# A decoder layer on one core: cross scores in two passes instead of three, and expert blocks issued among the last batches' steps

## The reference

```python
x = x + attn(layernorm(x), W_qkv, W_out)              # causal, window 64
x = x + xattn(layernorm(x), ctx, Wq, Wkv, Wo, bias)   # ctx: 375 rows per batch, bias by relative position
x = x + ffn(layernorm(x), ...)                        # 8 experts of width 512, top 2
# xattn: scores = q @ k.T + bias; softmax; @ v; @ Wo
# ffn: probs = softmax(x @ router.T), top 2 kept and renormalised
#      y = sum_e probs_e * ((silu(x @ gate_e + b) * (x @ up_e + b)) @ down_e + b)
```

## Time and profile before

| | us |
|---|---|
| median of three runs | 1296.43 |
| the profiled execution | 1294.94 |
| its span, first to last instruction | 1293.2 |
| PE busy | 1221.5 (94%) |
| DVE busy | 869.6 (67%) |
| POOL busy | 851.0 (66%) |
| ACT busy | 726.3 (56%) |

### The profile page before, as it was taken

One profiled execution on the slowest core, in us unless ns is written; L12 is line 12 of the kernel. 1 busy time (PEld: TensorE's weight loads), 2 busy tenths in 40 slices (PEclk: granted clock), 3 DMA queues, 4 the chain that ended last, 5 costly groups with the idle time before them and its releaser, 6 DMA issues. The chain is left out here.

```text
span 1293.2 us, 39996 instructions
## 1 busy us (share of the span) xinstructions
PE 1221.5 (94%) x13786; PEld 1084.2 (84%) x13787; DVE 869.6 (67%) x3942; ACT 726.3 (56%) x1822; POOL 851.0 (66%) x1595
## 2 busy tenths in 40 slices
PE   6899999999999999999999999996199999999996
PEld 4688888888888888888888888885199999999996
DVE  3567778787787877888778787786344444444443
ACT  3466666666666666666666666664054444444442
POOL 4677787887878878778787887765434444444443
PEclk8999999999999999999999999998599999999998
DMA  8700011100110111100111110101377322233222
GB/s 165 134 21 22 28 39 44 29 29 28 39 44 29 28 29 39 44 29 29 29 39 44 29 28 24 33 16 30 126 217 180 50 48 44 47 49 49 49 46 25
DMA packets 43957, 66.22 MB, mean 51 GB/s; under 512 B 6833, under 2 KB 30769, under 8 KB 43793
## 3 DMA queue, kind: packets, MB, share of 16 engines
q1 hardware_dynamic: 27808, 38.93, 11.4%
q0 software_dynamic: 15552, 25.05, 10.0%
q10 hardware_dynamic: 432, 0.10, 0.0%
HBM read 43.10 MB, written 20.95 MB: 50 GB/s over the span
## 5 line engine op out<-in xcount | busy, mean ns | idle before, releaser
L480 POOL TENSOR_SCALAR arena<-arena,mC 112x375 f32<-112x375 f32 x512 | 299.1, 595 | 117.6 <-DVE mC L888 117.4
L888 DVE CUSTOM_DVE_ANT_0 arena<-bank_S,arena 112x375 f32<-112x375 f32 x512 | 264.9, 543 | 90.7 <-PE bank_S L612 64.1
L1124 POOL DMA_INDIRECT out<-y,xb x63 | 114.8, 1822 | 206.2 <-DVE y L1270 165.4
L486 POOL TENSOR_SCALAR arena<-arena,mF 112x112 f32<-112x112 f32 x512 | 176.8, 362 | 23.1 <-DVE mF L876 21.4
L770 ACT ACTIVATE pTC<-bank_Q 126x336 f32<-126x336 f32 x286 | 128.6, 450 | 45.8 <-PE bank_Q L622 44.5
L734 ACT ACTIVATE arena<-bank_B 128x224 f32<-128x224 f32 (+5 forms) x229 | 87.5, 382 | 109.9 <-PE bank_B L541 35.1
L1257 DVE SCALAR_TENSOR_TENSOR hT<-bankU,gub,gate 128x128 f32<-128x128 f32 x252 | 71.0, 345 | 105.8 <-PE bankU L1166 93.7
L734 ACT ACTIVATE arena<-bank_A 128x224 f32<-128x224 f32 (+3 forms) x219 | 82.3, 376 | 96.7 <-PE bank_A L635 28.4
L622 PE MATMUL bank_Q<-ident,arena 112*126 112x112 f32 x858 | 130.9, 261 | 0.5 <-ACT pTC L770 0.5
L1166 PE MATMUL bankG<-xbT,gwb 128*128 128x128 f32 x1008 | 124.7, 277 | 1.0 <-ACT gwb L1213 1.0
L1207 ACT ACTIVATE xbT<-bankX 128x256 f32<-128x256 f32 x63 | 24.2, 384 | 178.1 <-PE bankX L1154 178.1
(11 more groups left out here) (207 smaller groups left out, 2919.3 us busy)
## 6 DMA issues: line engine op xcount, KB each, us to landing
arena<-in_l_ctxT SPq DMA_DIRECT2D x32, 378.0 KB, 3.6
xb<-xs POOLq DMA_DIRECT2D x63, 129.0 KB, 3.4
arena<-in_L_ffn_gate_w SPq DMA_DIRECT2D x8, 512.0 KB, 4.7
arena<-in_L_ffn_up_w SPq DMA_DIRECT2D x8, 512.0 KB, 5.7
arena<-in_L_ffn_down_w SPq DMA_DIRECT2D x8, 512.0 KB, 3.9
arena<-in_x SPq DMA_DIRECT2D x32, 112.0 KB, 2.2
out<-arena SPq DMA_DIRECT2D x32, 112.0 KB, 1.9
arena<-skew SPq DMA_DIRECT2D x8, 328.1 KB
```

Of the source, the lines that this page charges most:

```text
L480: pool.tensor_scalar(z[n % NZ][:, 0:T], z[n % NZ][:, 0:T], -1.0, mC[:, n:n + 1], ALU.mult, ALU.add).then_inc(s_u, 1)
L486: m = pool.tensor_scalar(sF[r][:, j, :], sF[r][:, j, :], -1.0, mF[:, r, j:j + 1], ALU.mult, ALU.add)
L888: dve.tensor_tensor_reduce(out=z[n % NZ][:, 0:T], in0=bank[f"S{r}"][0:S, 0:T], in1=nbias[:, n, :], scale=1.0, scalar=3.0e38, op0=ALU.add, ...
L1124: pool.indirect_dma_start(out=out[:, :], out_offset=bass.IndirectOffsetOnAxis(ap=xb[x][:, D + 1:D + 2].bitcast(I32), axis=0), in_=y2[x % 2 ...
```

## The change

1. **Two passes.** The high part of queries and keys is written to all partitions (`halves` without `hmask`, `keys_high` twice per half, once for each of two copies). A copy serves one head of a pair: there the partitions of the other head are then overwritten, by DMAs that SP issues, with the low part of the keys (step `kx`) and with the head's own queries (step `qx`). The partitions of a pair alternate now, so these DMAs step over every second partition. A matmul over 32 partitions then has 16 of high keys and 16 of low keys, and the two passes are high queries and low queries by those.
2. **A new `PERIOD`**, with `kx` and `qx` in it.
3. **A tail.** `TAIL_ORDER` is a list written out by hand of the last steps of the last batches, in which expert blocks 0 to 15 stand as `blk` (PE, ACT, DVE), `get` (POOL's loads) and `add` (POOL's adds), `pkg` (SP's weight loads, of which 0 to 9 stand ahead) and `pads`. One table, of the 42 blocks that the first 28 batches fill for certain, is made in `pfD` of batch 27; the other, of the remaining 21, in step `blocks` after block 6. The blocks use banks P (transposed rows), Q (down; one bank, before two), and S0 to S3 (gate, up); the second program is gone, and its loops begin at block 16.
4. The tiles are laid out anew in `arena`, so that the packages of experts 1 to 3, 4, and 5 to 7 each come free with a step. Expert 0's package is no longer loaded at the start but as `pkg:0` and `pkg:1`.

```diff
-                    for half in range(2):
-                        load_package(sp, 0, half)
...
+                        elif step == "kx":
+                            drained_wait(sp, "k0", b)
+                            drained_wait(sp, "k1", b)
+                            for p in range(2):
+                                sp.dma_start(k2[b % 2][1 - p:P:2, :, p, :].bitcast(F32),
+                                             k2_low[p:P:2, :, :].bitcast(F32)).then_inc(s_kx[b % 2], 16)
+                        elif step == "qx":
+                            drained_wait(sp, "q2", b)
+                            for p in range(2):
+                                sp.dma_start(q2[b % 2][1 - p:P:2, :, :, p, :].bitcast(F32),
+                                             q2[b % 2][p:P:2, :, :, p, :].bitcast(F32)).then_inc(s_qx[b % 2], 16)
...
+                        elif step == "get":
+                            if b == 0:
+                                pool.wait_ge(s_blocks, 1)
+                                buffers_free(pool)
...
+                            load(b, b)
+                        elif step == "add":
+                            add_and_load(b, b % XB)
...
-                        for u, w in PASSES:
+                        for u in range(2):
                             for r in range(HG):
-                                m = pe.matmul(bank[f"S{r}"][0:S, 0:T + 1], q2[b % 2][u][32 * r:32 * r + 32, c, k, :],
-                                              k2[b % 2][w][32 * r:32 * r + 32, c, :],
-                                              start=(u, w) == PASSES[0], stop=(u, w) == PASSES[-1])
+                                m = pe.matmul(bank[f"S{r}"][0:S, 0:T + 1], q2[b % 2][32 * r:32 * r + 32, u, c, p, :],
+                                              k2[b % 2][32 * r:32 * r + 32, c, p, :], start=u == 0, stop=u == 1)
...
+                        if step == "blk":
+                            if b == 0:
+                                for n in "PQ":
+                                    need(pe, drained[n], filled_last[n])
+                                need(pe, drained["S"], HG * filled_last["S"])
+                                transpose_in(0, 0, 0)
+                            expert_block(b, b % XB, b // XB)
...
-                        act.activation(k2[b % 2][0][:, o, :], B_[:, 0:T + 1], ACT.Copy).then_inc(s_kh, 1)
+                        for p in range(2):
+                            m = act.activation(k2[b % 2][:, o, p, :], B_[:, 0:T + 1], ACT.Copy)
+                        m.then_inc(s_kh, 1)
...
                             rows(b)
+                            if b == B1 - 1:
+                                drained_wait(dve, "pf", b)
+                                block_table(1)
+                        elif step == "blk":
+                            if b == 0:
+                                dve.wait_ge(s_blocks, 1)
+                                buffers_free(dve)
+                                weights(0, 0)
+                            expert_block(b, b % XB)
...
+pkg:10 pkg:11 pkg:12 pkg:13 pkg:14 pkg:15 blk:0 x3Tc:-1 pv3 pf:-2 oc3 pfD:-2 blk:1 add:0 otc nrmc sc:-2 blk:2
+add:1 onC rt:-1 oncc lg:-1 blk:3 add:2 woc re:-1 x2 st ln3 rcA:-1 rs3 x3 rcB:-1 blk:4 add:3 x3T pf:-1 x3Tc
+pfD:-1 blk:5 add:4 rt lg sc:-1 re rcA rcB blk:6 add:5 pf pfD blocks:2 sc pads blk:7 add:6 blk:8 add:7 blk:9
```

More of the change, by code:

```diff
@@ L87, in plan, with order @@
     return [(w, i + d) for i in range(-ahead, B + behind) for w, d in ORDER if 0 <= i + d < B]
+def order(B):
+    steps = [s for s in plan(B) if s not in TAIL_STEPS(B)]
+    return steps + [s for s in ((w, j) if w in ALONE else (w, B - 1 + j) for w, j in TAIL)]
 def fills(steps):
@@ L146, in decoder_layer @@
             PK += width
[L148 removed]
+        arena = sb("arena", [P, E * PK])
         packages = arena[:, 0:E * PK].rearrange("p (e k) -> p e k", e=E)
@@ new lines, in decoder_layer, with s0 @@
+            v2 = [s1(f"v2_{i}", [TP, TC, H, HP]) for i in range(2)]
+            with ExitStack() as early:
+                def s0(name, shape):
+                    return sb(name, shape, F32R, early)
+                cT = [s0(f"cT_{part}", [P, DC, TPAD]) for part in ("high", "low")]
+                wkv = [s0(f"wkv_{part}", [P, DC, 2 * D]) for part in ("high", "low")]
+                q2 = [s0(f"q2_{i}", [P, 2, DC, 2, S]) for i in range(2)]
+                k2 = [s0(f"k2_{i}", [P, DC, 2, T + 1]) for i in range(2)]
+                k2_low = s0("k2_low", [P, DC, T + 1])
@@ new lines, in gate_or_up @@
+                    def gate_or_up(j, q, part, copied, bk, read, then):
+                        pe.wait_ge(s_cX, j + 1)
+                        if not back(j - 1):
+                            pe.wait_ge(read, j - 1)
+                        pe.wait_ge(copied, j + 1)
+                        w = part[q].rearrange("p (c f) -> p c f", c=DC)
+                        for f in range(FC):
+                            for c in range(DC):
+                                m = pe.matmul(bk[q][:, f * P:(f + 1) * P], w[:, c, f * P:(f + 1) * P], xbT[q][:, c, :],
+                                              start=(c == 0), stop=(c == DC - 1))
+                        m.then_inc(then, 1)
@@ new lines, in down @@
+                    def down(j, q):
+                        e = pe.value_load(blocks[0:1, 1, bass.ds(j, 1)], min_val=0, max_val=E - 1)
+                        pe.wait_ge(s_hh, j + 1)
+                        if not back(j):
+                            pe.wait_ge(s_yb, j)
+                        w = package(e, "dw").rearrange("p (c d) -> p c d", c=FC)
+                        for c in range(FC):
+                            m = pe.matmul(bankY[:, 0:D], hT[q][:, c, :], w[:, c, :], start=(c == 0), stop=(c == FC - 1))
+                        m.then_inc(s_y, 1)
@@ L950, in _, with expert_block @@
+                    def expert_block(j, x, last=False):
+                        if not last:
+                            weights(j + 1, 1 - x % 2)
+                        hidden(j, x % 2)
+                        if not (isinstance(j, int) and j == 0):
+                            weigh_rows(j - 1, (x - 1) % XB)
                     for step, b in steps:
```

607 lines of the change are left out of this document (310 added, 297 removed).

## The result

The changed kernel took 1291.51 us (median of 7 runs, 1289.34 to 1293.21) against 1296.43 for the kernel before in the same set: a ratio of 0.9962, 95% interval 0.9950 to 0.9974. Forecast were 1251 us and a range of 1238 to 1268. The profiled execution has a span of 1290.6 us, before 1293.2.

What follows compares the result with a forecast made beforehand. PE alone was taken to bound batches and blocks, apart from start-up, hole and end. Terms -22.4 + 2 + 1.6 - 29.4 + 3.0 = -45.2 us from 1294.94 gave 1249.7, forecast as a 1251 median, range 1238 to 1268.

Steps and rivals of the forecast that it cites:

- Passes: Score steps of all batches: 128 matmul passes removed at 0.175 us each on PE, -22.4 us.
- Order pitch: Batch periods: the same 48 PE steps in a new order, +1.6 us, bounds of 8 either way.
- Short waits: Batch periods: PE waits at score banks because DVE's reserve shrinks, +2 us, bounds 0 and 22.
- paired loads: Batch periods: the new DMAs for queries and keys land before they are wanted, no charge.
- the late queries: Rival: PE waits at each S0 for the paired queries, kernel slower at about 1370 us; chance 0.05.
- Start: Start of the kernel: expert 0's package leaves the queue, paired DMAs join it; 0 us, bounds 4 either way.
- Hole: Between last batches and expert blocks: of 41 us lost, blocks between the steps win back 29.4 us.
- the tables' waits: First table in full batches costs 3.0 us; at the second, PE waits 4.3 us for block 8's up weights.
- the clock at 1.00 through what was the hole: Tail: expected sign that PE's granted clock stays full where blocks now fill the idle stretch.
- The two rules of the Trainium skill: DMA pieces under 512 bytes become read-modify-writes; each table load adds a 1.38 us drain. Neither changed the forecast.
- The hole back in part: Rival, tail: tables and adds at upper bounds hold PE, 15 us return, 1266 us; chance 0.14.
- The signs of being wrong: PE waiting on q or k at every S0, period staying 26.9, or over 25 us idle before block 16.

Runs made afterwards that it cites:

- e3: The changed kernel with the second pass of every cross score step issued twice: 1308.72 us, 1.0086 of the kernel before.
- e1: The changed kernel with the load of batch 3's x issued ahead of the late weights and the skewed bias: 1279.66 us, 0.9860 of the kernel before.
- set 5: Later runs, without pauses, of the changed kernel unchanged (1266.47 us, 0.9787 of the kernel before) and of e19.
- e13: The changed kernel with batch 3's x loaded early, table instructions spread over steps, paddings one behind each add: 1249.47 us; again in a set with pauses, 1268.33.
- e19: e13 with p10 (3 transposes) moved between pvS and pv0: 1258.36 us, 0.9711 of the kernel before.

## Why the prediction was wrong, step by step

- **Passes**, -22.4: right. 0.172 us each (e3), and the four steps gave 0.96 us a period instead of 0.70. The surplus is a wait that S1 had in the kernel before. "PE had not one gap a period before" overlooked it: the trace has one of 0.21 us in each, in front of pvS, and it is gone.

```profile
423.84 0.97 PE L570 MATMUL bank_A<-arena 112*32 112x112 f32 x32 [0.21 <-DVE run L927]
```

- **Order pitch**, +1.6 (8 either way): right for what it priced. Without the pauses everything but the score steps takes 23.84 us a period, before 23.85. **What failed here is a term that isn't there:** in the set of the result the pause in pv0 adds 0.70 us a period, 17 us in the body, and the sum has nothing for it. The trace of before showed no such pause, so it could hardly be foreseen; its cause stays open.
- **Short waits, paired loads, the late queries**: right in that TensorE waits for no DMA in the body; the rival at 1370 is out. The 2 us of short waits weren't seen.
- **Start, 0 with 4 either way: failed.** The step looked only at what the change takes out of SP's queue and adds to it. It has no word of ln1 one batch further ahead of nrm, which makes VectorE, and behind it all, wait for a load that stands behind the bias. Measured 13.1 (9.4 and 10.2 in two later profiles); the one load is worth 11.9 (e1).
- **Hole, -29.4: failed in size.** Blocks do fill it, and the tables' waits are as priced (4.29 and 3.81 against 3.0 and 4.3). Of the 19.2 us missed, 6.7 are the difference to the tail without pauses (487.2 against 480.5). In the 12.5 left, the step that failed is that the slow clock was put at nothing ("the clock at 1.00 through what was the hole"): behind waits of 1 to 4 us TensorE ran at half the clock, 1.7 us lost three times and some 1.5 twice, 8.1 in all by this estimate; set 5's profile comes to about 8 as well. TensorE's busy time in this part points the same way: 449.4 us before, 455.5 now and 452.3 without pauses, though the passes took 3.8 off. The rest, some 4 us, isn't settled. The wait for the last x differs from profile to profile (2.09 us here, 0.45 in set 5, where the gate behind it takes 2.02 us, not 3.53). Spreading the tables gets 3.9 back (e13's tail 476.6 against 480.5).
- **The two rules of the Trainium skill that the prediction cites**: of the small pieces, 448 bytes in the queries' pair, the trace shows no harm (no wait for them in the body); the keys' pair, which lands in 2.3 us, says nothing about them, since its pieces are 1504 bytes. And the drain behind a table load isn't seen: the load at 911.80 takes 1.28 us, and the silu starts at 913.09. Neither decided anything.
- **Which rival came true**: none. "The hole back in part", 1266, has the right sign in the tail, but the pauses, worth 25 us between the changed kernel's two kinds of set (1291.5 and 1289.5 against 1266.5), and the start were in no rival. The signs of being wrong didn't show either: no wait on q or k, a period under 26.9, and under 25 us idle from the last batch to block 16.
- **Where the forecast would have held, it is in part luck.** Without pauses the kernel takes 1266.5, inside the range, but start and tail miss their terms by 12.6 and 12.5 us there, and the body gains 9.2 more than forecast (23.3 instead of 14.1).

The kernel before hardly feels the kind of set: 1296.4 to 1297.6 with pauses elsewhere, 1294.9 and 1295.3 without. So the change made the kernel more sensitive: 0.4% better in the one, 2.1% in the other. What makes a set one or the other was not found. That TensorE's instructions come too late in a row of small matmuls is argued, not shown: the packets of the instruction queue come every 10 us or so in both kinds (20 in 200 us of the changed kernel, 21 in e13), and the pause stands at the same place in every batch. The best version is e13, which beats both in either kind: 1268.33 and 1249.47.

## What to carry to other kernels

When a table of steps moves a consumer ahead, look up where its load stands in the DMA queue at the start, before the steady state: one 112 KB load behind 2.6 MB cost 12 us. Price a hole that is filled by what is left in it and by the slow clock behind each wait that stays. And take an edit's worth from more than one set of runs where the profile shows "issue" time at a fixed place.

## What was unexpected of the hardware

- 56 small matmuls in a row (32 and 24) ran in 1.48 us, or in 2.18 us with a pause after some 35, in one and the same program, and all kernels of a set of runs agreed in it.
- Eight indirect DMAs in a row on GpSimd, 1.27 us apart, went with pauses on issue of other engines (12.5 us on ScalarE) in the same sets only.
- Three transposing matmuls between two rows of small ones (pvS and pv0) cost 0.34 us a period more than the same three behind both (e19).
- After waits of 1 to 4 us the granted clock fell to half, and 16 matmuls took 3.5 to 3.8 us instead of 1.95.
